# A four-layer cross-attention kernel on one core: layers 0 and 1 interleaved pair by pair, layer 1 two streams behind, and norms outside layer 1 averaged in one product

## What is computed

```python
x = L0(x, ctx)       # RMS norm of x and of ctx; cross attention (heads of 64, 4 key/value heads); x + out
x = L1(x, ctx)       # norm, self attention; norm, cross attention; norm, gated GELU network; heads of 16,
                     # q, k, v and the probabilities rounded to 8 bits ("fake quantised")
x = L2(x, ctx, ctx)  # norm, cross attention (heads of 64, 16 key/value heads); norm, relu network
x = L3(ctx, x)       # norm, causal self attention; norm, cross attention; norm, relu network; heads of 16
```

## Time and profile before

| what | value |
|---|---|
| median of 3 runs | 5082.05 us (5082.0 to 5082.79) |
| the profiled execution | 5084.24 us, span of its instructions 5082.1 us |
| PE, PE weight loads | busy 4750.2 us (93%), 3575.8 us (70%) |
| DVE, ACT, POOL | busy 2947.2 (58%), 2834.6 (56%), 2125.3 us (42%) |
| mean granted PE clock | 0.970 |
| matmul records | 34496 |
| transfers | 103.09 MB, mean 20 GB/s |

### The profile page before, as it was taken

The page is one execution under the profiler, slowest core; times in us unless marked ns, Lnnn a source line. Parts: engine busy times, 40 slices in busy tenths (PEclk is TensorE's granted clock), DMA queues, the critical chain, the costliest instruction groups (busy, mean ns, idle before and its releaser), DMA issues.

```text
span 5082.1 us, 91660 instructions
## 1 busy us (share of the span) xinstructions
PE 4750.2 (93%) x34496; PEld 3575.8 (70%) x34496; DVE 2947.2 (58%) x6697; ACT 2834.6 (56%) x9058; POOL 2125.3 (42%) x4307
## 2 busy tenths in 40 slices
PE   8999999977878777889999999999999999999998
PEld 5666666656666666667777777777777777887777
DVE  5555555556665656664444445444445777677765
ACT  4555555688888888873333333333333666666664
POOL 2333333487787878771111111111112444444443
PEclk9999999989898988999999999999999999999999
DMA  2000000000000000001000000000000000000000
GB/s 81 20 20 23 20 24 23 24 27 20 11 21 14 17 18 14 18 30 39 14 11 14 14 14 11 14 14 14 11 22 24 33 21 18 21 18 17 21 16 7
DMA packets 40040, 103.09 MB, mean 20 GB/s; under 512 B 4912, under 2 KB 21552, under 8 KB 38192
## 3 DMA queue, kind: packets, MB, share of 16 engines
q1 hardware_dynamic: 39600, 97.23, 5.9%
HBM read 82.53 MB, written 14.68 MB: 19 GB/s over the span
## 4 chain that ended last, share of the span: by engine, by line
PE 79%; ACT 9%; POOL 8%; DVE 2%; issue 2%; DMA 0%; SPq 0%; ACTq 0%; DVEq 0%
PE ring L1268 47%; PE ring L1219 11%; PE score L1200 10%; ACT e L1378 5%; POOL e L1735 4%; PE ring L1250 3%; PE ring L1243 3%; POOL e L1745 2%; PE ring L1257 2%; PE ring L1216 1%; DVE nmax L1513 1%; POOL rsumw L1728 1%; POOL work L1721 1%; ACT probs L1418 1%; PE score L1195 1%
## 5 line engine op out<-in xcount | busy, mean ns | idle before, releaser
L1738 POOL TENSOR_SCALAR e<-e,rsum 112x375 f32<-112x375 f32 (+1 forms) x2048 | 1080.8, 546 | 2611.6 <-DVE rsum L1520 2606.2
L1418 ACT COPY probs<-ring 125x336 f32<-125x336 f32 (+1 forms) x997 | 413.0, 448 | 1530.3 <-PE ring L1219 1470.5
L1513 DVE TENSOR_REDUCE nmax<-score 112x2 f32<-112x750 f32 (+1 forms) x1152 | 1057.2, 950 | 328.2 <-PE score L1200 327.6
L1378 ACT ACTIVATE e<-score,nmax 112x375 f32<-112x375 f32 (+1 forms) x2048 | 1038.7, 539 | 88.3 <-DVE nmax L1513 86.5
L1268 PE MATMUL ring<-h,weights 128*128 128x224 f32 x3840 | 903.4, 370 | 5.5 <-ACT h L1350 3.0
L1268 PEld LDWEIGHTS ring<-h,weights 128*128 128x128 f32 x3840 | 712.2, 197 | 77.7 <-issue 27.0
L1219 PEld LDWEIGHTS ring<-consts,e 112*125 112x125 f32 x4608 | 594.0, 189 | 231.1 <-issue 172.8
L1200 PE MATMUL score<-keys,q 64*112 64x375 f32 (+2 forms) x3584 | 559.1, 491 | 162.8 <-ACT e L1378 150.6
L1219 PE MATMUL ring<-consts,e 112*125 112x112 f32 x4608 | 659.9, 279 | 9.3 <-POOL e L1738 4.8
L1378 ACT ACTIVATE e<-score,nmaxc,quant 112x375 f32<-112x375 f32 (+1 forms) x1024 | 555.1, 554 | 10.7
L1268 PE MATMUL ring<-weights,ctx 128*125 128x256 f32 (+1 forms) x1536 | 551.2, 488 | 0.1
(11 more groups left out here) (120 smaller groups left out, 5858.7 us busy)
## 6 DMA issues: line engine op xcount, KB each, us to landing
ctx<-ctx_t SPq DMA_DIRECT2D x128, 375.0 KB, 2.9
out_t<-x SPq DMA_DIRECT2D x64, 224.0 KB, 1.9
x<-out_t SPq DMA_DIRECT2D x48, 224.0 KB, 2.5
weights<-weights SPq DMA_DIRECT2D x7, 1024.0 KB, 5.6
x<-x_t SPq DMA_DIRECT2D x16, 224.0 KB, 2.5
weights<-weights SPq DMA_DIRECT2D x1, 3328.0 KB, 12.0
weights<-weights SPq DMA_DIRECT2D x1, 2304.0 KB, 9.1
weights<-weights SPq DMA_DIRECT2D x1, 2048.0 KB, 7.2
```

The lines of the kernel that those rows point to most:

```text
L1378: ins = nc.scalar.activation(e_of(u)[:, n * width:(n + 1) * width], score_bank(u)[0:S, n * width:(n + 1) * width], ACT.Exp, bias=minus, sc ...
L1418: ins = nc.scalar.copy(dst, src)
L1513: ins = dve.tensor_reduce(to, src, AX, ALU.max, negate=True)
L1738: ins = nc.gpsimd.tensor_scalar(mine, mine, rsum[0:S, slot(u), n:n + 1], 0.0, ALU.mult, ALU.add)
```

## The change

Layers 0 and 1 are interleaved. At step t layer 0 works on stream t, layer 1 on stream t - 2 (cross attention) and t - 1 (self attention). Within a step the string `STEPS` sets the order of the pairs: `a` is a layer 0 pair, `c` a layer 1 cross pair, `s` a layer 1 self pair. Steps 0 and 1 hold layer 0 (and the first self attention), steps 2 to 15 both layers, steps 16 and 17 layer 1 alone. x stays in its slot between the two layers: 16 stores and 16 loads go. The weights, the keys, values, heads and probabilities of both layers get places side by side; layer 0 has one heads buffer instead of two, the context one buffer per layer, and the gates of layer 1 share the buffer `hidden`. Only layers 2 and 3 keep their scores in fours. Outside layer 1 POOL first adds the two halves of the channels (`fold`, `foldsq`, `cfold`), and PE needs one product instead of two.

```diff
-QUADS = (0, 1, 2, 3)
+QUADS = (2, 3)
+LAG = 2
+STEPS = "acacacacacaca" "aa" "scacscacsccs" "acacacaca"
...
     def place_attention(self):
-        for layer in range(4):
+        for t in range(STREAMS + LAG):
+            zero, one, own = t, t - LAG, t - LAG + 1
+            there = lambda s: 0 <= s < STREAMS
+            if t < LAG:
+                steps = "a" * 16 + "ssss"
+            elif t == LAG:
+                steps = "a" * 10 + "cccccc" + "sccsccsccs" + "acacacacaa"
+            elif t == STREAMS - 1:
+                steps = "a" * 8 + "c" + "a" * 8 + "scsccscs" + "c" * 11
+            elif t >= STREAMS:
+                steps = "cscsccscs" + "c" * 11
+            else:
+                steps = STEPS
+            left = {"a": self.sets(0, "cross", zero) if there(zero) else [],
+                    "c": self.sets(1, "cross", one) if there(one) else [],
+                    "s": self.sets(1, "self", own) if there(own) else []}
...
         for n in self.norms:
             j = self.var_of[n]
-            self.add("square", n, "A", 0.58, j.pos - 0.6)
+            if n.layer > 1:
+                self.add("fold", n, "G", 0.5, self.mean_of[n].pos - 0.4)
+            self.add("square", n, "A", 0.58, j.pos - 0.8)
+            if n.layer != 1:
+                self.add("foldsq", n, "G", 0.5, j.pos - 0.4)
...
     def residual(self, j):
         if j.m == 0:
-            return []
+            return self.every(0, "o", s=j.s) if j.layer == 1 else []
...
     def heads_users(self, o):
...
+        if o.layer == 0:
+            return self.every(0, "o", s=o.s - 1) if o.s else []
...
         def tensor_product(pe, wait, j, ps):
             if j.kind == "mean":
-                x_loads(wait, layer, j.s)
-                wait.saves(plan.residual(j))
-                return product(ps[:, 0:N], ((mean_w[:, :], x_of(j)[:, k, :]) for k in range(KC)))
+                if layer == 1:
+                    x_loads(wait, layer, j.s)
+                    wait.saves(plan.residual(j))
+                    return product(ps[:, 0:N], ((mean_w[:, :], x_of(j)[:, k, :]) for k in range(KC)))
+                wait.wait_ge(folded, nth["fold", j.norm])
+                return pe.matmul(ps[:, 0:N], mean_w[:, :], squares[:, j.norm.index % 2, 0, :], start=True, stop=True)
...
         def pool_program(pool):
             for kind, x_ in plan.order["G"]:
+                if kind == "fold":
+                    n = x_
+                    x_loads(wait, n.layer, n.s)
+                    wait.saves(plan.residual(plan.mean_of[n]))
+                    if n.index >= 2:
+                        wait.done([plan.var_of[plan.norms[n.index - 2]]])
+                    to = squares[:, n.index % 2, 0, :]
+                    nc.gpsimd.tensor_tensor(to, x_of(n)[:, 0, :], x_of(n)[:, 1, :], ALU.add).then_inc(folded, 1)
+                    continue
...
+                if kind == "cfold":
+                    wait.wait_ge(ctx_squared, nth["csquare", x_])
+                    to = ctx_sq[:, 0, :]
+                    nc.gpsimd.tensor_tensor(to, to, ctx_sq[:, 1, :], ALU.add).then_inc(ctx_folded, 1)
+                    continue
```

More of the change, by code:

```diff
@@ L204, in place_attention @@
     def place_attention(self):
-        for layer in range(4):
+        for t in range(STREAMS + LAG):
[14 more added lines that the diff above has]
+                    "s": self.sets(1, "self", own) if there(own) else []}
+            left = {name: [o for o in os for _ in range(2)] for name, os in left.items()}
+            for name in steps:
+                if left[name]:
+                    self.pair_of(left[name].pop(0))
+            assert not any(left.values())
@@ L206, in place_attention @@
+        for layer in (2, 3):
             for s in range(STREAMS):
[L207 to L210, removed]
-                else:
-                    own = [(layer, "self", s + 1, b, 0) for b in (2 * s + 2, 2 * s + 3)] if s < STREAMS - 1 else []
-                    places = (0, 1)
+                cross = self.sets(layer, "cross", s)
+                if layer == 2:
+                    own, places = (self.sets(3, "self", 0) if s == STREAMS - 1 else []), (2, 4)
+                else:
+                    own, places = (self.sets(3, "self", s + 1) if s < STREAMS - 1 else []), (0, 2)
@@ L214, in place_attention @@
                 for i, o in enumerate(cross):
[L215 to L221, removed]
+                    self.set_of(o)
+                    if own and i in places:
+                        self.set_of(own[places.index(i)])
@@ L417, in list_steps @@
             for s in range(STREAMS):
[L418 removed]
+                if layer:
+                    self.add("store", (layer, s), "D", 2.0, self.at[layer, "f2", s, 0, 1].pos + 0.5)
         for s in range(STREAMS):
@@ L447, in own_values_end, with zero_user @@
+        self.add("zero", "own", "G", 2.0, max(j.pos for j in self.jobs if j.layer == 1) + 2.0)
+    def zero_user(self, slot):
+        return [u for u in range(129, 129 + VS) if u % VS == slot][0]
     def own_values_end(self):
@@ L487, in before @@
                 yield "job", self.var_of[self.norms[x.index - 2]]
+        elif kind == "fold":
+            yield "x", (x.layer, x.s)
+            for i in self.residual(self.mean_of[x]):
+                yield "save", i
+            if x.index >= 2:
+                yield "job", self.var_of[self.norms[x.index - 2]]
+        elif kind == "foldsq":
+            yield "square", x
+        elif kind == "cfold":
+            yield "csquare", x
         elif kind == "scale":
@@ L599, in frees @@
                 yield "job", i
-            if j.of.layer == 2 and j.of.s == 1:
-                for i in self.every(1, "up", s=STREAMS - 1):
-                    yield "save", i
         elif j.kind in ("q", "q2"):
@@ L1770, in sync_program @@
                     g = stream(layer, s)
-                    wait.saves(every(layer, "f2" if layer else "o", s=s))
+                    wait.saves(every(layer, "f2", s=s))
                     sp.dma_start(out[s], x[:, g % XS, :, :]).then_inc(x_stored[g % XS], 16)
```

357 lines of the change are left out of this document (208 added, 149 removed).

## The result

The changed kernel takes 5024.73 us (median of 4 runs, 5022.57 to 5027.41) against 5082.02: ratio 0.9887, 95% interval 0.987 to 0.9905, so 57 us are gained. Faster was right; 4880 was 145 us too low, and the time lies 15 us above the upper end of the range, 5010.

A forecast was written before the change was run, and what follows sets the result against it. PE was taken to bound layers 0, 2 and 3, no single engine layer 1. From 5082 us, interleaving gave -151, edges +6 and norms -57, so 4880 us, with a range of 4730 to 5010.

The forecast's parts named there:

- T = 131: Length in us of each of the 14 steps that interleave layers 0 and 1; both layers together 2118 us, -151 us.
- rest 1.4: In a full step: 1.4 us taken of the 4 us that the group count missed in layer 1.
- 16 pairs add 0 to 2.4 us; I take 0.8: Layer 1's scores in twos instead of fours: PE's added load in a full step, taken as 0.8 us.
- Nine groups of four pairs: Full step cut into groups: PE needs 115 us; with larger needs of other engines in four groups, sixth included, 127.6 us.
- Eight to sixteen records at half speed: PE's work behind the sixth group of a full step runs at the lower clock, costing 1.5 to 3 us, taken as 2.
- Edges: Steps 1 and 15 add some 20 us, the steps of layer 1 alone save about 14: +6 us.
- Norms: Layers 2 and 3: 160 products less on PE at 0.38 us each, 61 us, taken as -57 us.
- At nothing: Dropped stores and loads of x, one context buffer per layer, one heads buffer in layer 0: no cost; 40 us if one showed.
- A: Forecast case for the interleaved steps: T between 126 and 136 us, program 4810 to 4950 us; 55%.
- C: Rival for the interleaved steps: layer 1's coupling stays, ratio 1.21 to PE's 117, T = 142, program 5034 us; 20%.
- B: Rival for the interleaved steps: PE is fed throughout, lagging jobs fill light places, T = 118, program 4698 us; 18%.
- D: Rival for the interleaved steps: the ring of four banks delays each job 0.15 us, T = 153, program 5188 us; 7%.

The follow-up runs named there:

- e10: Changed kernel with another STEPS string that puts the four self pairs of a step next to each other, same work: 5161.46 us.
- e6: Changed kernel with another STEPS string that spreads the four self pairs over the full step, same work: 4941.12 us.
- e13: Changed kernel with pairs placed two by two and self pairs spread far apart in the full steps, scores in twos: 4861.07 us.
- e3: Changed kernel with pairs placed two by two (aacc instead of acac, self pairs two by two), scores still in twos: 5013.06 us.
- e4: e3 with scores in fours in all layers: 5024.09 us.
- e14: e13 with scores in fours in all layers: 4909.39 us.
- e11: Changed kernel with the planner's old estimates for an exponential (2.9 and 1.3) in layers 2 and 3: 5003.05 us.
- e1: Kernel before with only the folds and single products for the norms outside layer 1, no interleaving: 5021.74 us.
- e8: Changed kernel with layer 3's mean again in two products on PE and no fold of x there: 5023.18 us.

## Why the prediction was wrong

The mechanism is the one that the runs show: PE's load, plus the idle time of a light place, plus the lower clock behind it (e10, e6 and e13 move only that place). What failed are sizes: PE's load in a step was put 8 us too low, above all by the price of scores in twos (0.8 us for a measured 4.9 to 5.7), and the half-speed work at 2 us for 6.1. Outside the step, layer 3's gain failed, by the planner's estimates.

**The step, T = 131, measured 138.2.** By the terms of the prediction:

| term | forecast | measured |
|---|---|---|
| PE's work (the groups' 115; 117 by loads) | 115 | 123.7 |
| idle: groups 12.6, rest 1.4 | 14.0 | 8.4 |
| extra busy time at half clock | 2 | 6.1 |
| sum | 131 | 138.2 |

- *"16 pairs add 0 to 2.4 us; I take 0.8"* is the largest miss, and its bound failed too: it left out the self pairs and layer 0. The argument "four concurrent ones already ran at 0.075 each" was wrong: two take as long as four. Measured are 4.9 to 5.7 us (e3 against e4, e13 against e14; 4.5 by rows).
- *"862.45 of 1092 us at clock 0.89, which at full clock is 58 us"* was 1.6 too low. The mean clock counts idle time too, and part of the low clock lay on idle time; in windows of 3 us the work is 59.6. With the 4.9 of the twos this takes the loads from 117 to 123.5. That T was built on the groups' 115 and not on the loads' 117 is 2 more. (The loads of ACT, POOL and DVE, 98, 86 and 87, were right: 96.4, 85.4 and 84.8 by the windows above. The last has a slip of 1 in its sum.)
- *Nine groups of four pairs* found the right place, the sixth group: 6.0 us of lacking work (10.4 - 4.4) against 5.2 us of waits there in the step shown. The other three groups, 6.5 us forecast, hardly show: 2.8 us of waits in the rest of that step. Why they are covered was not tested. The rest term of 1.4 has nothing of its own to show for it. That idle time was put 5.6 too high hid part of the two errors beside it, which is luck.
- *"Eight to sixteen records at half speed", 2 us:* the windows show two of 6.9 us at 0.50 and part of one before, with 49 and 39 records in the two; the extra is 6.1 us.
- *PE busy about 90% at a clock near 0.96, idle before scores, ended by ACT, with POOL near full:* it was 94% at 0.94. The place and ACT are right, POOL is not. It was busy 3.99 to 5.90 of 6.90 us there, ACT 6.83.

So T made 14 x 7.2 = 101 of the 145 us. Edges made 2 and layer 3 made 39; layer 2 gave 1 more than forecast. The last 4 are the median over the span of the profiled execution (5024.7 against 5020.8), where the kernel before had none.

**Edges, +6.** The end of layer 1 is 103 us later than forecast (42 instead of 145), 101 of them by 14 times the miss of a full step: right within 3. Only 12 of the 14 steps hold the plain string, so the split between the two terms is rough.

**Norms, -57.** Layer 2's 24 us came. Layer 3's 33 did not, and it took 6 more, for a reason outside the term: the planner's estimates, which the prediction doesn't price. PE's work did fall there, from 69.9 to 67.3 us a stream (windows of 3 us), but idle time rose from 1.3 to 3.2 and 0.7 came from a lower clock. With the old estimates (e11) layer 3 gives 25 of the 33. The folds hold no PE in layers 2 and 3, as said (e1, e8), though each takes 0.66 us on POOL, not 0.5.

**At nothing.** The stores, loads and buffers showed in no list of PE's waits that was read.

**Rivals.** The time lies between A (up to 4950) and C (5034). C's mechanism, a ratio of layer 1 (1.21) that the mix keeps, is refuted by e13: its step is 124.2 for 123.5 of work. B's holds for another order, with a step of 124, not 118. D's ring does not decide: e13 runs its jobs at 99% through the same four banks.

The Trainium skill ("TensorE: Matmul & The Clock Gate", section "A second HAM failure mode: psum-queue depth-cycling") says that frequent short idling of PE between groups of matmuls makes the clock swing between its two levels and costs throughput. The traces agree: the clock is 0.94 with one light place a step, 0.90 in e10, 1.00 in e13.

## What to carry to other kernels

Before two stages are mixed, sum the load of the bounding engine with every price that the mixing changes; a narrower group of concurrent products can take as long as a wide one, and that alone can eat the gain. Then look for the one stretch of the order in which that engine has least to do: there the step is decided, and moving a few pairs was worth 26 us of 150 with no work changed. A busy time is made comparable between two clocks in short windows, not by one mean clock. And read each estimate that a planner uses as part of the change: two of them cost 30 us in a layer that the change was not about, 22 in all.

## What the runs showed of the hardware

- Two bf16 score products of 32 rows and 375 columns run side by side hold PE for 0.30 us, four of them for 0.30 as well.
- In the changed kernel the granted clock went to 0.50 behind a window with PE busy 3.59 of 6.90 us and was still 0.50 in a window with PE busy 6.90 of 6.90. Twelve small products a step in the pauses brought the mean clock from 0.94 to 0.99; they cost 4.0 us of work a step, and the time fell by only 9 us.
- Four float32 score records of 64 rows and 375 columns hold PE for 1.52 us at a granted clock of 0.50 and for 0.82 us at 1.00.
- GpSimd's addition of two 128x224 operands takes 0.66 us, against 0.37 for one input of the same shape:

```profile
L1821 POOL TENSOR_TENSOR squares<-x x80: 651/657/666, 2146.4 to 4994.8; 128x224 f32<-128x224 f32 x80
```
